# Setting up the folded weights of a tokenizer: query bias in two more columns, one semaphore for each bias, key projection ahead of the bias of V

## The chip, the cores and the metric

The kernel runs on one core of a Trainium2 chip. The metric is the device time of one launch in microseconds, the median of several executions. The kernel before takes 2070.14 us (median of 3 executions, 2069.56 to 2070.2).

## What is computed

The input is x, 2 batches of 4096 tokens of width 256, in float32. Three stages follow each other: a tokenizer with linear attention scores and a gate, an attention in which each token attends across the batch of 2, and a feed-forward part for the half of the tokens that a router picks. Only the first is touched by the change:

```
q = x @ Wq + bq
k = x @ Wk + bk
v = x @ Wv + bv
scores = jnp.einsum('btd,bsd->bts', q, k)
retained = jnp.einsum('bts,bsd->btd', d_gamma_batched * scores, v)
y = retained @ Wo + bo
out = jnp.where(y >= 0, y, prelu_a * y)
```

The kernel doesn't form q, k and v. It folds the weights once: A = Wk·Wqᵀ takes the place of the two projections in the score (x A xᵀ), Wv·Wo that of the value projection and the output projection, and the biases become a column added to the folded key (from Wq and bk), one extra column of the folded value (from Wk and bq, the term of the score that depends on the key token alone) and a row added to the value (from bv and Wo).

## The kernel before

It is written for one core with a program for each engine and semaphores between them: what stands in an engine's program is done in that order. The DMAs are issued by SP (SyncE), in its program's order too. Matrix products take float32 values in two halves: for each operand ScalarE (ACT) makes a rounded copy "hi" and VectorE (DVE) the rest "lo" = value minus hi, and TensorE (PE) does three products, hi·hi, hi·lo and lo·hi.

`setup_weights` (line 73) runs once, at the start of the launch. SP loads, in this order: the weights wqT, wkT, wvT and wo (256 KB each), the first chunk of x (512 KB, into x32), then two copies each of bq, bk and bv as columns (lines 98 to 101: four bytes per partition and half), the column of bo, and gamma, beta, attn_bo, prelu and wr, each a row that is copied to all 128 partitions. All of the biases and rows but wr count on one semaphore, `loaded`. PE forms the product pa = A (line 159, two banks) as soon as wqT and wkT are there, then pv = Wv·Wo (line 165). After that it waits for `rows`, with the bias products behind it: DVE makes bq_rows and bv_rows (a bias spread over 128 columns, lines 132 and 134), and waits ahead of them for all of `loaded`:

```
dve.wait_ge(loaded, 16 * n_loads)
...
pe.wait_ge(rows, 2 * KD)
```

Then PE does wkT·bq (line 171, into two more columns of pv), wqT·bk (line 174), bv_rows·wo (line 177) and bq_rows·bk (line 180), and only the last of these counts `prod` up, upon which DVE copies bk_col, vo_f and v_bias out of PSUM (lines 137 to 140), ACT makes vo_hi and DVE vo_lo. In between DVE has copied A out (a_f, line 122), ACT has split it (a_hi) and the first x (x_hi), and DVE made a_lo and x_lo. In float32 without halves, as in these set-up products, one matmul of the program stands in the trace as two records.

`tokenizer` (line 195) follows, for each of the two batches: `project` for 8 chunks of 512 tokens, then `attend` for 8 chunks. In `project`, PE does 12 matmuls of 512 columns with a_hi and a_lo (line 635: the folded key, two banks) and then 24 of 258 columns with vo_hi and vo_lo (line 648: the folded value, four banks); ACT and DVE copy the banks out with the bias and split them again. PE's first projection stands behind the bias products in its program. SP loads the x of a chunk two chunks ahead and, in chunk 0, the first four tiles of the gate. `attend` is the long part: per chunk 32 rounds of scores (line 678) and sums over values (line 663), with the gate streamed in. After the tokenizer come the attention weights, the mixing and the feed-forward part, which the change leaves alone.

Of the kernel before, what the change touches and what calls it, by code (L numbers as in the profile page):

```python
# [5 lines left out]
P = 128  # L6
# [9 lines left out]
F32 = mybir.dt.float32  # L16
# [56 lines left out]
def setup_weights(pr, W, ident, work):  # L73
# [3 lines left out]
    with ExitStack() as ctx:  # L77
        wqT, wkT, wvT, wo = (sb(nc, ctx, n, [P, KD, D]) for n in ("wqT", "wkT", "wvT", "wo"))
        bq2, bk2, bv2 = (sb(nc, ctx, n, [P, KD, 2]) for n in ("bq2", "bk2", "bv2"))
# [3 lines left out]
        pa, pv, (pb, pr_) = pr.banks[0:2], pr.banks[2:4], pr.banks[4:6]  # L83
        qk_loaded, vo_loaded, loaded, made, rows, prod, kept, hi_ok, lo_ok = (
            pr.sem("w_" + n) for n in ("qk_loaded", "vo_loaded", "loaded", "consts", "rows", "products", "kept",
                                       "hi", "lo"))
        n_loads = 3 * 2 + 1 + 4
# [4 lines left out]
        @block.sync  # L92
        def _(sp):
            for t, name, sem in ((wqT, "tok_WqT", qk_loaded), (wkT, "tok_WkT", qk_loaded),
                                 (wvT, "tok_WvT", vo_loaded), (wo, "tok_Wo", vo_loaded)):
                sp.dma_start(t[:, :, :], ins[name].rearrange("(k p) n -> p k n", p=P)).then_inc(sem, 16)
            sp.dma_start(x32, ins["xT"][0, 0]).then_inc(x_ld, 16)
            with nc.allow_non_contiguous_dma(reason="bias columns, once"):
                for t, name in ((bq2, "tok_bq"), (bk2, "tok_bk"), (bv2, "tok_bv")):
                    for j in range(2):  # L100
                        sp.dma_start(t[:, :, j], ins[name].rearrange("(k p) -> p k", p=P)).then_inc(loaded, 16)
                sp.dma_start(W["bo_col"][:, :], ins["tok_bo"].rearrange("(k p) -> p k", p=P)).then_inc(loaded, 16)
            sp.dma_start(W["gamma"][:, :], ins["attn_gamma"].partition_broadcast(P)).then_inc(loaded, 16)
            sp.dma_start(W["beta"][:, :], ins["attn_beta"].partition_broadcast(P)).then_inc(loaded, 16)
            sp.dma_start(W["attn_bo"][:, :], ins["attn_bo"].partition_broadcast(P)).then_inc(loaded, 16)
            sp.dma_start(W["prelu"][:, :], ins["tok_prelu_a"].partition_broadcast(P)).then_inc(loaded, 16)
            sp.dma_start(W["wr"][:, :], ins["ffn_wr"].partition_broadcast(P)).then_inc(pr.sem("wr_ld"), 16)

        @block.gpsimd
        def _(pool):  # L110
# [4 lines left out]
                                    base=0, pattern=[[-1, P]], channel_multiplier=1).then_inc(made, 1)  # L115

        @block.vector
        def _(dve):

            for j in range(KD):  # L120
                dve.wait_ge(prod, j + 1)
                nc.vector.tensor_copy(a_f[:, j, :], pa[j][:, 0:D]).then_inc(kept, 1)
            dve.wait_ge(hi_ok, 1)
            nc.vector.tensor_tensor(W["a_lo"][:, :, :], a_f[:, :, :], W["a_hi"][:, :, :].bitcast(F32),
                                    ALU.subtract).then_inc(lo_ok, 1)
            dve.wait_ge(x_hi_ok, 1)
            nc.vector.tensor_tensor(W["x_lo"][:, 0], x32, W["x_hi"][:, 0].bitcast(F32), ALU.subtract).then_inc(x_lo_ok, 1)
            dve.wait_ge(loaded, 16 * n_loads)
            dve.wait_ge(made, 3)

            for k in range(KD):
                nc.vector.tensor_scalar(bq_rows[:, k, :], ones[:, :], bq2[:, k, 0:1], None,
                                        ALU.mult).then_inc(rows, 1)
                nc.vector.tensor_scalar(bv_rows[:, k, :], ones[:, :], bv2[:, k, 0:1], None,
                                        ALU.mult).then_inc(rows, 1)
# [1580 lines left out]
```

## Time and profile before

| | |
|---|---|
| median of 3 executions | 2070.14 us |
| the profiled execution | 2072.95 us, of which its span is 2071.2 us |
| PE busy | 1988.7 us (96% of the span) |
| DVE, ACT, POOL busy | 1222.2, 675.0 and 451.0 us |
| bytes moved by DMA | 250.14 MB, mean 121 GB/s |
| chain that ended last, by engine | PE 90%, DVE 4%, issue 2%, ACT 2%, POOL 1% |
| costliest lines | L678 (scores) and L663 (values), 34% of the chain each |
| mean granted PE clock | 0.977 of full speed |

The page of the profile shows busy time for each engine and, in 40 slices, when. The chain of waits is followed back from the last instruction; it says which work the end hangs on. The timeline lists instructions in order of time, with the idle time of the engine before each in brackets and what ended it.
### The profile page before, as it was taken

What the parts mean: (1) busy time and instruction counts of PE and PEld (TensorE: products, weight loads), DVE (VectorE), ACT (ScalarE), POOL (GpSimd) and SP (SyncE); (2) the same over time, 40 slices, a digit from 0 to 9 for tenths busy, and PEclk for the clock granted to TensorE, in tenths of its full rate; (3) what the DMA queues carried; (4) which work ended last, traced back from release to release, by engine and by line L of the source; (5) the groups of instructions that cost most, each with busy time, mean ns of one, the idle gap of its engine ahead of it and who ended that gap; (6) DMA issues with size and microseconds to landing.
All of it is one profiled execution on the core that took longest, in us unless ns stands there. A gap on an engine that the chain in (4) does not pass through costs nothing.

```text
span 2071.2 us, 27479 instructions
## 1 busy us (share of the span) xinstructions
PE 1988.7 (96%) x9534; PEld 1646.7 (80%) x9534; DVE 1222.2 (59%) x2220; ACT 675.0 (33%) x1093; POOL 451.0 (22%) x578
## 2 busy tenths in 40 slices
PE   7999999999999999999999999999999989829998
PEld 6888888888888888888888888888887878718897
DVE  4656565665656556656565665656554358756553
ACT  4422222222222225422222222222222147524454
POOL 3302020202202023312020201202023057532342
PEclk9999999999999999999999999999999989959999
DMA  4232433334243333242433334243334469620110
GB/s 143 88 105 73 162 112 122 112 122 145 75 164 112 122 112 132 72 153 81 154 112 123 111 122 150 73 162 112 112 112 143 148 241 313 220 77 22 42 42 31
DMA packets 88114, 250.14 MB, mean 121 GB/s; under 512 B 11968, under 2 KB 32448, under 8 KB 88000
## 3 DMA queue, kind: packets, MB, share of 16 engines
q1 hardware_dynamic: 84928, 240.27, 34.5%
q0 software_dynamic: 3072, 8.44, 1.3%
q8 instruction: 61, 1.00, 0.2%
q14 instruction: 53, 0.43, 0.1%
HBM read 194.05 MB, written 54.62 MB: 120 GB/s over the span
## 4 chain that ended last, share of the span: by engine, by line
PE 90%; DVE 4%; issue 2%; ACT 2%; POOL 1%; DMA 0%; SPq 0%; DVEq 0%; ACTq 0%; POOLq 0%
PE bank L663 34%; PE bank L678 34%; PE bank L1568 4%; PE bank L810 4%; PE bank L1588 4%; PE bank L713 3%; PE bank L1169 2%; PE bank L635 1%; PE bank L609 1%; PE bank L619 1%; DVE kt L482 0%; DVE vf L493 0%; PE bank L648 0%; ACT work L380 0%; PE bank L836 0%
## 5 line engine op out<-in xcount | busy, mean ns | idle before, releaser
L678 PE MATMUL bank<-x_hi,kt 128*128 128x512 f32 x2048 | 724.0, 395 | 1.5 <-DVE work L519 1.4
L519 DVE SCALAR_TENSOR_TENSOR work<-bank,d_col,gate 128x512 f32<-128x512 f32 x512 | 383.8, 750 | 553.7 <-PE bank L678 544.7
L398 ACT ACTIVATE p_hi<-work 128x512 fp32r<-128x512 f32 x512 | 324.1, 633 | 1065.5 <-PE bank L663 1024.9
L678 PEld LDWEIGHTS bank<-x_hi,kt 128*128 128x128 f32 x2048 | 384.4, 188 | 90.4 <-DVE work L519 2.4
L663 PE MATMUL bank<-p_hi,v_hi 128*128 128x512 f32 x1024 | 407.0, 397 | 0.3 <-ACT yT L360 0.2
L663 PE MATMUL bank<-p_hi,v_lo 128*128 128x512 f32 x1024 | 404.2, 395 | 0.0
L663 PE MATMUL bank<-p_lo,v_hi 128*128 128x512 f32 x1024 | 403.4, 394 | 0.0
L678 PE MATMUL bank<-x_lo,kt 128*128 128x512 f32 x1024 | 401.0, 392 | 0.0
L507 DVE TENSOR_TENSOR p_lo<-work,p_hi 128x512 fp32r<-128x512 f32 x512 | 367.4, 718 | 29.3 <-ACT p_hi L398 29.2
L568 POOL TENSOR_SCALAR spread<-mv 128x4 f32<-128x4 f32 x16 | 4.9, 308 | 1125.4 <-DVE mv L451 1125.4
L663 PEld LDWEIGHTS bank<-p_hi,v_hi 128*128 128x128 f32 x1024 | 192.2, 188 | 50.6 <-DVE p_lo L507 5.3
L663 PEld LDWEIGHTS bank<-p_hi,v_lo 128*128 128x128 f32 x1024 | 192.3, 188 | 46.3
L663 PEld LDWEIGHTS bank<-p_lo,v_hi 128*128 128x128 f32 x1024 | 193.2, 189 | 44.7
L678 PEld LDWEIGHTS bank<-x_lo,kt 128*128 128x128 f32 x1024 | 192.3, 188 | 43.4
L1534 DVE TENSOR_TENSOR act_lo<-act,act_hi 128x512 fp32r<-128x512 f32 x64 | 59.2, 925 | 91.0 <-ACT act_hi L1472 90.8
L1568 PE MATMUL bank<-ffn,act_hi 128*128 128x256 f32 x512 | 97.4, 289 | 0.0
L1588 PE MATMUL bank<-fx_hi,ffn 128*128 128x512 f32 x256 | 92.5, 408 | 2.2 <-DVE fx_lo L1483 2.2
L1568 PEld LDWEIGHTS bank<-ffn,act_hi 128*128 128x128 f32 x512 | 84.2, 194 | 4.3 <-DVE act_lo L1534 0.2
L575 POOL TENSOR_TENSOR mn_sb<-mn_sb,gamma 128x256 f32<-128x256 f32 x64 | 55.2, 893 | 98.7 <-DVE mn_sb L456 98.7
L1568 PE MATMUL bank<-ffn,act_lo 128*128 128x256 f32 x256 | 73.6, 288 | 0.0
L713 PE MATMUL bank<-kt 128*128 128x256 f32 (+1 forms) x384 | 68.3, 339 | 2.2 <-DVE kt L544 2.2
L713 PEld LDWEIGHTS bank<-kt 128*128 128x128 f32 x384 | 59.2, 189 | 11.2 <-DVE kt L544 2.9
(226 smaller groups left out, 2271.7 us busy)
## 6 DMA issues: line engine op xcount, KB each, us to landing
gate<-in_gateT SPq DMA_DIRECT2D x256, 512.0 KB, 3.6
work<-in_xT SPq DMA_DIRECT2D x32, 512.0 KB, 4.7
scratch_rows<-rows SPq DMA_DIRECT2D x16, 518.0 KB, 4.0
scratch_h<-work SPq DMA_DIRECT2D x16, 512.0 KB, 3.0
scratch_mn<-mn_sb SPq DMA_DIRECT2D x16, 512.0 KB, 6.8
scratch_mT_hi<-mT_hi SPq DMA_DIRECT2D x16, 512.0 KB, 2.7
scratch_mT_lo<-mT_lo SPq DMA_DIRECT2D x16, 512.0 KB, 4.0
gate<-scratch_mn SPq DMA_DIRECT2D x16, 512.0 KB, 4.2
```

The costliest lines, as they stand in the source:

```text
L398: nc.scalar.activation(p_hi[:, i % 2, :], p32[:, i % RP, :], ACT.Copy).then_inc(hi_done, 1)
L507: nc.vector.tensor_tensor(p_lo[:, i % 2, :], p32[:, i % RP, :], p_hi[:, i % 2, :].bitcast(F32), ALU.subtract).then_inc(lo_done, 1)
L519: nc.vector.scalar_tensor_tensor(p32[:, i % RP, :], S[i % 2][:, :], d_col[:, i:i + 1], gate[:, g % RG, j, :], ALU.add, ALU.mult).then_inc( ...
L575: nc.gpsimd.tensor_tensor(mn_sb[:, j, :], mn_sb[:, j, :], W["gamma"][:, :], ALU.mult).then_inc(scaled, 1)
L663: mm = pe.matmul(Y[m][:, :], v, p, start=i == 0 and n == 0, stop=i == ST - 1 and n == 2)
L678: mm = pe.matmul(S[i % 2][:, :], w, x, start=n == 1, stop=n == 3 * KD)
L713: mm = pe.matmul(out, w, x, start=early(c, 1) and j == 0 and n == 0, stop=False, skip_group_check=True)
L810: mm = pe.matmul(bank[:, :], ww, x, start=i == 1, stop=i == 3 * pr.KD)
L1169: mm = pe.matmul(products[:, j, 0:D + 2], x, w, start=i == 0, stop=i == 3 * KD - 1)
L1534: nc.vector.tensor_tensor(a_lo[:, j % 2, :], act32[:, j % 2, :], a_hi[:, j % 2, :].bitcast(F32), ALU.subtract).then_inc(al_ok, 1)
L1568: mm = pe.matmul(YB[t // 2][:, (t % 2) * D:(t % 2 + 1) * D], a, w, start=j == 0 and t % 2 == 0 and n == 0, stop=j == FT - 1 and n == 2, sk ...
L1588: mm = pe.matmul(HB[j % 2][:, :], w, x, start=n == 1, stop=n == 3 * KD)
```

## The change

- The query bias gets two more columns behind the query weights: a tile wq_b of width D + 2 in place of wqT, with bq loaded into columns D and D + 1. The product of line 159 becomes 258 columns wide (line 157 of the changed kernel), and its last two columns are wkT·bq. The matmuls of line 171 are gone.
- Each set of bias columns has a semaphore (bq_ld, bk_ld, bv_ld) and is loaded by ACT's DMA queue at the start, five DMAs; bv once. x comes third on SP's queue, ahead of wvT and wo.
- The spread rows bq_rows and bv_rows are made by POOL, not by DVE.
- wqT·bk (line 163) stands before wvT·wo (line 169). The two products with the spread rows are a function `value_bias` that is called in PE's program behind the first key projection, ahead of the first value projection.
- bo's column, gamma, beta, attn_bo, prelu and wr are loaded in chunk 0 of `project`, behind the first four gate tiles, on a semaphore w_rows_ld that DVE waits for behind the last chunk of `project`.
- DVE makes x_lo before a_lo, and ACT x_hi before a_hi.

```diff
-        pa, pv, (pb, pr_) = pr.banks[0:2], pr.banks[2:4], pr.banks[4:6]
+        pa, pv, (pb, pr_) = pr.banks[0:2], pr.banks[2:4], pr.banks[6:8]
...
         @block.sync
-            for t, name, sem in ((wqT, "tok_WqT", qk_loaded), (wkT, "tok_WkT", qk_loaded),
-                                 (wvT, "tok_WvT", vo_loaded), (wo, "tok_Wo", vo_loaded)):
-                sp.dma_start(t[:, :, :], ins[name].rearrange("(k p) n -> p k n", p=P)).then_inc(sem, 16)
+            for t, name in ((wq_b[:, :, 0:D], "tok_WqT"), (wkT[:, :, :], "tok_WkT")):
+                sp.dma_start(t, ins[name].rearrange("(k p) n -> p k n", p=P)).then_inc(qk_loaded, 16)
             sp.dma_start(x32, ins["xT"][0, 0]).then_inc(x_ld, 16)
+            for t, name in ((wvT, "tok_WvT"), (wo, "tok_Wo")):
+                sp.dma_start(t[:, :, :], ins[name].rearrange("(k p) n -> p k n", p=P)).then_inc(vo_loaded, 16)
...
         @block.gpsimd
+            pool.wait_ge(bq_ld, 32)
+            pool.wait_ge(bv_ld, 16)
+            for k in range(KD):
+                nc.gpsimd.tensor_scalar(bq_rows[:, k, :], ones[:, :], wq_b[:, k, D:D + 1], None, ALU.mult).then_inc(rows, 1)
+                nc.gpsimd.tensor_scalar(bv_rows[:, k, :], ones[:, :], bv1[:, k, 0:1], None, ALU.mult).then_inc(rows, 1)
...
         @block.vector
             for j in range(KD):
                 dve.wait_ge(prod, j + 1)
+                nc.vector.tensor_copy(vo_f[:, j, D:D + 2], pa[j][:, D:D + 2])
                 nc.vector.tensor_copy(a_f[:, j, :], pa[j][:, 0:D]).then_inc(kept, 1)
+            dve.wait_ge(x_hi_ok, 1)
+            nc.vector.tensor_tensor(W["x_lo"][:, 0], x32, W["x_hi"][:, 0].bitcast(F32), ALU.subtract).then_inc(x_lo_ok, 1)
             dve.wait_ge(hi_ok, 1)
...
-            dve.wait_ge(loaded, 16 * n_loads)
...
+            dve.wait_ge(prod, KD + 3)
+            nc.vector.tensor_copy(W["v_bias"][:, :], pr_[:, 0:D + 2]).then_inc(kept, 1)
+            dve.wait_ge(kept, 2 * KD + 2)
...
         @block.scalar
+                for t, name, sem in ((wq_b[:, :, D], "tok_bq", bq_ld), (wq_b[:, :, D + 1], "tok_bq", bq_ld),
+                                     (bk2[:, :, 0], "tok_bk", bk_ld), (bk2[:, :, 1], "tok_bk", bk_ld),
+                                     (bv1[:, :, 0], "tok_bv", bv_ld)):
+                    act.dma_start(t, ins[name].rearrange("(k p) -> p k", p=P)).then_inc(sem, 16)
...
         @block.tensor
             pe.wait_ge(qk_loaded, 32)
+            pe.wait_ge(bq_ld, 32)
...
+                    mm = pe.matmul(pa[j][:, 0:D + 2], wkT[:, k, j * P:(j + 1) * P], wq_b[:, k, :], start=k == 0,
...
                     if early(c, 1):
+                        if b == 0:
+                            value_bias(pe)
                         pe.wait_ge(w_lo, 2)
```

PE's program from its first instruction to the first projection, before (a row is one or, with xN, N matmuls of the program; a_hi, a_lo are the halves of A, vo_hi, vo_lo those of Wv·Wo):

```order
L159 MATMUL bank<-wqT,wkT 128x256 x4
L165 MATMUL bank<-wo,wvT 128x256 x4
L171 MATMUL bank<-bq,wkT 128x2 x2
L174 MATMUL bank<-bk,wqT 128x2 x2
L171 MATMUL bank<-bq,wkT 128x2 x2
L174 MATMUL bank<-bk,wqT 128x2 x2
L177 MATMUL bank<-wo,bv_rows 128x256 x2
L180 MATMUL bank<-bk,bq_rows 128x2 x2
L602 UNCONDITIONAL_BRANCH
L635 MATMUL bank<-x_hi,a_hi 128x512
```

The same stretch of PE's program in the changed kernel, in two pieces, up to the first projection and from its last matmul on:

```order
L157 MATMUL bank<-wq_b,wkT 128x258 x4
L163 MATMUL bank<-bk,wq_b 128x2 x4
L169 MATMUL bank<-wo,wvT 128x256 x4
L609 UNCONDITIONAL_BRANCH
L642 MATMUL bank<-x_hi,a_hi 128x512
```

```order
L642 MATMUL bank<-x_hi,a_lo 128x512
L175 MATMUL bank<-wo,bv_rows 128x256 x2
L177 MATMUL bank<-bk,bq_rows 128x2 x2
L657 MATMUL bank<-vo_hi,x_hi 128x258
L657 MATMUL bank<-vo_lo,x_hi 128x258
```

Two products with the spread rows have moved from ahead of the 12 matmuls of the first key projection to behind them, wqT·bk from behind wvT·wo to ahead of it, and the two products with bq alone are gone.

DVE's program at the start, before:

```order
L122 COPY a_f<-bank 128x256 x2
L124 TENSOR_TENSOR a_lo<-a_f,a_hi 128x512
L127 TENSOR_TENSOR x_lo<-work,x_hi 128x1024
L132 TENSOR_SCALAR bq_rows<-ones_setup,bq 128x128
L134 TENSOR_SCALAR bv_rows<-ones_setup,bv 128x128
L132 TENSOR_SCALAR bq_rows<-ones_setup,bq 128x128
L134 TENSOR_SCALAR bv_rows<-ones_setup,bv 128x128
L137 COPY bk_col<-bank 128x2
L139 COPY vo_f<-bank 128x258 x2
L140 COPY v_bias<-bank 128x258
L142 TENSOR_TENSOR vo_lo<-vo_f,vo_hi 128x516
```

And DVE's program at the start in the changed kernel:

```order
L118 COPY vo_f<-bank 128x2
L119 COPY a_f<-bank 128x256
L118 COPY vo_f<-bank 128x2
L119 COPY a_f<-bank 128x256
L121 TENSOR_TENSOR x_lo<-work,x_hi 128x1024
L123 TENSOR_TENSOR a_lo<-a_f,a_hi 128x512
L126 COPY bk_col<-bank 128x2
L129 COPY vo_f<-bank 128x256 x2
L131 TENSOR_TENSOR vo_lo<-vo_f,vo_hi 128x516
L134 COPY v_bias<-bank 128x258
```

The four spread rows have left DVE, x_lo stands ahead of a_lo, two copies of two columns are new, and v_bias is copied last.

## Rows read from the trace of the kernel before

**Rows 1.** The page: busy us, share of the span and instructions of each engine.

```profile
PE 1988.7 (96%) x9534; PEld 1646.7 (80%) x9534; DVE 1222.2 (59%) x2220; ACT 675.0 (33%) x1093; POOL 451.0 (22%) x578
```

**Rows 2.** Chain of waits, first 110 us: start us, us, what.

```profile
8.83 6.65 DMA prelu<-in_tok_prelu_a
...
16.43 1.01 PE bank L171 x4
...
22.56 4.11 PE bank L635 x12
```

**Rows 3.** Timeline of PE: start us, us, instruction, records; brackets: idle before it.

```profile
4.49 3.69 PE L159 MATMUL bank<-wqT,wkT 128*128 128x256 f32 x8 [4.49 <-DMA wkT<-in_tok_WkT]
8.02 1.89 PE L165 MATMUL bank<-wo,wvT 128*128 128x256 f32 x8
16.43 1.01 PE L171 MATMUL bank<-bq,wkT 128*128 128x2 f32 x4 [6.52 <-DVE bv_rows L134]
17.30 0.99 PE L174 MATMUL bank<-bk,wqT 128*128 128x2 f32 x4
...
19.86 2.06 PE L177 MATMUL bank<-wo,bv_rows 128*128 128x256 f32 x4
...
22.42 0.77 PE L635 MATMUL bank<-x_hi,a_hi 128*128 128x512 f32 x1
...
25.09 0.40 PE L635 MATMUL bank<-x_hi,a_hi 128*128 128x512 f32 x1
...
26.50 0.28 PE L648 MATMUL bank<-vo_hi,x_hi 128*128 128x258 f32 x1
...
29.39 0.40 PE L635 MATMUL bank<-x_hi,a_hi 128*128 128x512 f32 x1
```

**Rows 4.** Windows: stretch, its length, each engine's busy us, then PEclk, DMA share, GB/s.

```profile
14.70:14.80 0.10, 0.00 (x0) 0.00 (x0) 0.00 (x0) 0.00 (x0) 0.00 (x0) 0.94 1.03 400
...
16.40:20.00 3.60, 3.57 (x17) 3.57 (x17) 0.00 (x0) 0.00 (x0) 0.00 (x0) 0.50 1.03 420
20.00:25.00 5.00, 5.00 (x15) 4.16 (x15) 1.86 (x5) 1.54 (x2) 0.00 (x0) 0.50 0.39 158
...
30.00:60.00 30.00, 30.00 (x189) 26.95 (x188) 22.07 (x36) 23.34 (x45) 20.29 (x41) 1.00 0.26 84
```

**Rows 5.** Timeline of DVE at the start.

```profile
8.22 0.42 DVE L122 COPY a_f<-bank 128x256 f32<-128x256 f32 x1 [1.19 <-PE bank L159]
9.34 0.69 DVE L124 TENSOR_TENSOR a_lo<-a_f,a_hi 128x512 fp32r<-128x512 f32 x1 [0.70 <-ACT a_hi L148]
10.29 1.22 DVE L127 TENSOR_TENSOR x_lo<-work,x_hi 128x1024 fp32r<-128x1024 f32 x1 [0.26 <-ACT x_hi L150]
...
22.68 0.75 DVE L139 COPY vo_f<-bank 128x258 f32<-128x258 f32 x2
```

**Rows 6.** Timeline of ACT at the start.

```profile
9.21 1.04 ACT L150 ACTIVATE x_hi<-work 128x1024 fp32r<-128x1024 f32 x1
23.46 0.64 ACT L152 ACTIVATE vo_hi<-vo_f 128x516 fp32r<-128x516 f32 x1 [13.21 <-DVE vo_f L139]
```

**Rows 7.** DMA issues in the first 60 us: count, KB each, us to landing.

```profile
bq<-in_tok_bq SPq DMA_DIRECT2D x2, 1.0 KB, 4.8
```

**Rows 8.** Line 97, load of the first x, issued at 2.82 us.

```profile
DMA to landing us min/median/max: 5.6/5.6/5.6
```

**Rows 9.** DMA from 7.5 to 8.0 us, the bias columns: packets, MB, share of 16 engines.

```profile
q1 hardware_dynamic: 774, 0.04, 105.3%
```

**Rows 10.** Groups of POOL instructions: count, busy us, mean ns, idle before.

```profile
L579 POOL TENSOR_TENSOR mn_sb<-mn_sb,beta 128x256 f32<-128x256 f32 x64 | 64.7, 1042 | 0.0
```

**Rows 11.** Timeline of all engines, first 60 us: SP's and POOL's start.

```profile
0.81 0.44 SPq L96 DMA_DIRECT2D wqT<-in_tok_WqT  x1
...
1.39 0.29 POOL L114 TENSOR_SCALAR_AFFINE_SELECT ident<-ident 128x128 f32<-128x128 f32 x1 [0.25 <-POOL ones_setup L112]
...
3.33 0.95 SPq L101 DMA_DIRECT2D bq<-in_tok_bq  x2
```

More of the change, by code:

```diff
@@ L82, in setup_weights @@
         a_f, vo_f = sb(nc, ctx, "a_f", [P, KD, D]), sb(nc, ctx, "vo_f", [P, KD, D + 2])
-        pa, pv, (pb, pr_) = pr.banks[0:2], pr.banks[2:4], pr.banks[4:6]
[L84 to L87, printed above, removed]
+        pa, pv, (pb, pr_) = pr.banks[0:2], pr.banks[2:4], pr.banks[6:8]
+        (qk_loaded, vo_loaded, bq_ld, bk_ld, bv_ld, made, rows, prod, kept, hi_ok, lo_ok) = (
+            pr.sem("w_" + n) for n in ("qk_loaded", "vo_loaded", "bq_ld", "bk_ld", "bv_ld", "consts", "rows", "products",
+                                       "kept", "hi", "lo"))
         x_ld, x_hi_ok, x_lo_ok = pr.sem("xp_ld0"), pr.sem("xp_hi"), pr.sem("xp_lo")
@@ L125, in _ @@
                                     ALU.subtract).then_inc(lo_ok, 1)
-            dve.wait_ge(x_hi_ok, 1)
-            nc.vector.tensor_tensor(W["x_lo"][:, 0], x32, W["x_hi"][:, 0].bitcast(F32), ALU.subtract).then_inc(x_lo_ok, 1)
-            dve.wait_ge(loaded, 16 * n_loads)
[L129 to L135, printed above, removed]
             dve.wait_ge(prod, KD + 1)
             nc.vector.tensor_copy(W["bk_col"][:, :], pb[:, 0:2 * KD:2]).then_inc(kept, 1)
+            dve.wait_ge(prod, KD + 2)
             for j in range(KD):
-                nc.vector.tensor_copy(vo_f[:, j, :], pv[j][:, 0:D + 2]).then_inc(kept, 1)
-            nc.vector.tensor_copy(W["v_bias"][:, :], pr_[:, 0:D + 2]).then_inc(kept, 1)
+                nc.vector.tensor_copy(vo_f[:, j, 0:D], pv[j][:, 0:D]).then_inc(kept, 1)
             dve.wait_ge(hi_ok, 2)
@@ L156, in _ @@
             pe.wait_ge(qk_loaded, 32)
+            pe.wait_ge(bq_ld, 32)
             for j in range(KD):
                 for k in range(KD):
-                    mm = pe.matmul(pa[j][:, 0:D], wkT[:, k, j * P:(j + 1) * P], wqT[:, k, :], start=k == 0,
+                    mm = pe.matmul(pa[j][:, 0:D + 2], wkT[:, k, j * P:(j + 1) * P], wq_b[:, k, :], start=k == 0,
                                    stop=k == KD - 1)
                 mm.then_inc(prod, 1)
+            pe.wait_ge(bk_ld, 32)
+            for j in range(KD):
+                for k in range(KD):
+                    mm = pe.matmul(pb[:, 2 * j:2 * j + 2], wq_b[:, k, j * P:(j + 1) * P], bk2[:, k, :],
+                                   start=j == 0 and k == 0, stop=k == KD - 1, skip_group_check=True)
+            mm.then_inc(prod, 1)
             pe.wait_ge(vo_loaded, 32)
@@ L182, in _ @@
             last.then_inc(prod, 1)
+        return value_bias
 def gram_view(work, D):
@@ L310, in project @@
                             load_gate(0, b * NC, g)
+                    if early(c, 1) and b == 0:
+                        for n, name in (("gamma", "attn_gamma"), ("beta", "attn_beta"), ("attn_bo", "attn_bo"),
+                                        ("prelu", "tok_prelu_a")):
+                            sp.dma_start(W[n][:, :], ins[name].partition_broadcast(P)).then_inc(pr.sem("w_rows_ld"), 16)
+                        with nc.allow_non_contiguous_dma(reason="a bias column, once"):
+                            sp.dma_start(W["bo_col"][:, :], ins["tok_bo"].rearrange("(k p) -> p k", p=P)).then_inc(
+                                pr.sem("w_rows_ld"), 16)
+                        sp.dma_start(W["wr"][:, :], ins["ffn_wr"].partition_broadcast(P)).then_inc(pr.sem("wr_ld"), 16)
                 chunks(sp, b, project)
```

43 lines of the change are left out of this document (14 added, 29 removed).

## Prediction

> **What bounds the kernel now.** I read the busy times of the page first: PE works in 96% of the span and no other engine in more than 59% [rows 1]. So the launch is PE's work one after the other, and a change gains only what PE waits for or does slowly. The change lies in the set-up. The chain of waits says what holds the start: a DMA, the load of prelu, which lands at 15.5 us, then the bias products from 16.43 us, then the first projection, line 635 [rows 2]. None of the products behind the wait needs prelu, or the three broadcast rows ahead of it; they hang on it because all count on one semaphore. In PE's timeline the reader sees the hole: work from 4.49 us, idle for 6.52 us before line 171, the first projection at 22.42, the first value product (line 648) at 26.50 [rows 3]. From there the projections run without a gap, PE 30.00 of 30 us busy [rows 4]. That start, 26.50, is the number to follow: what comes behind it is the same work in the same order, and I let it shift as a whole.
>
> The same rows show two speeds. Line 159 has 8 records from 4.49 until line 165 starts at 8.02, a pitch of 0.44 us for 256 columns; line 165 has the same shape and goes through 8 in 1.89, 0.236 each [rows 3]. So the clock rose from 1.2 to 2.4 GHz close to 8.0. It fell within 14.7 to 14.8, with PE idle since 9.91, and stood at 0.50 until about 25 [rows 4]: six of the twelve first projections went at 0.445 (22.42 to 25.09), six at 0.235 (25.09 to 26.50) [rows 3].
>
> **The change, part by part.**
>
> *Start of PE.* Before, PE starts when wkT has landed, 4.49 [rows 3]. Now it waits for both columns of bq too. They are the first two issues of ACT's queue. No row shows a DMA issued by ACT; SP issues such a column in 0.48 (0.95 for two) and its queue begins at 0.81 [rows 11], so I let the second go out at 1.29. A bq column took 4.8 us to land, behind five large loads on one queue [rows 7]; that gives an upper end of 1.29 + 4.8 = 6.1. The lower end is 4.49, if the columns are there before wkT. A column is 256 packets of four bytes, and 774 small packets took all 16 engines 0.5 us [rows 9], so a column takes 0.17. If bq and bk pass between the packets of wqT and wkT, wkT is late by up to 4 · 0.17 = 0.7; with the two of bq, by 0.35. I take 4.9, near the lower end, since the columns have a queue without a backlog; the range keeps 4.49 to 6.1. The Trainium skill (DMA: Bandwidth & Descriptors, Rules for kernel authors) says that spreading DMAs over the issuing engines saves only issue time, since all run on the same 16 engines and interleave. By that rule the columns do delay wkT and 4.9 is right; if the queues did not share, it would be 4.49 and the whole sum 0.4 better.
>
> *PE's own products.* Line 157: 8 records, 258 instead of 256 columns, 3.53 · 258/256 = 3.56 at the low clock, until 8.46. The two more columns cost 0.03 us and do away with 8 records of line 171, at a pitch of 0.22 (16.43 to 17.30 for four [rows 3]) 1.7 us. Line 163: 8 two-column records, 0.22 each at 1.2 GHz; at 2.4 GHz nothing shows them, between 0.11 (half) and 0.22; I take 0.11, since nothing but the clock would hold them: 0.9, until 9.4. Line 169: 8 · 0.236 = 1.9 at 2.4 GHz, until 11.3. Its operand wo is now the last of the five large loads, the place that x had, which landed at 2.82 + 5.6 = 8.4 [rows 8]; with five columns in between (5 · 0.17) 9.3, just under 9.4. That cover is thin: each us beyond costs one.
>
> *A and x in halves.* The second a_f copy started 0.2 us after line 159's last record, at 8.22 [rows 5]; now 8.7. Two two-column copies are added, one in the wait for the second product, one at under 0.42 ahead of a_f; say 9.1 for a_f's end. Then x_lo, 1.22, and a_lo, 0.69 [rows 5]: 11.0. x_hi (1.04 [rows 6]) must be ready by 9.1: x is third on the queue instead of fifth, so not later than 8.4, and x_hi ends by 9.5 at the latest, x_lo by 10.7, a_lo by 11.4. So DVE and PE end together, DVE 0.3 ahead. Before, a_lo and x_lo ended at 11.5 [rows 5], to no use.
>
> *First projection.* It starts at 11.3 instead of 22.42. If the clock rose at the end of line 157 and stays, 12 · 0.235 = 2.8, until 14.1; before, 4.08.
>
> *Bias of V.* Behind it value_bias: 4 records of 256 columns and 4 of two, 4 · 0.236 + 4 · 0.11 = 1.4, until 15.5. It waits for the spread rows, from POOL. No POOL row has this shape; between a 128x128 select at 0.29 [rows 11] and a tensor-tensor of 128x256 at 1.04 [rows 10], four take 1.2 to 4.2. The third bias, fifth on ACT's queue, goes out by 0.81 + 5 · 0.48 = 3.2 and at 4.8 lands by 8.0, so the rows stand by 12.2, under 14.1. POOL has nothing else to do there.
>
> *Value halves.* vo_f follows line 169: 11.3 + 0.75 for two copies [rows 5], vo_hi 0.64 [rows 6], vo_lo 0.7: 13.5, under 15.5. The copy of v_bias waits for value_bias, and queued behind it on DVE is x_lo of chunk 1: 15.6 + 0.4 + 1.2 = 17.2. PE wants that after 24 value products, (29.39 − 26.50) = 2.9 [rows 3], at 18.4. The first vf copies stand behind x_lo too, some 0.8 later against line 648 than before; four banks take that up, and DVE is busy for 22 of 30 us there [rows 4], so it catches up.
>
> *Rows loaded late.* Six issues, 0.48 each, 2.9 on SP's queue behind the gate tiles and ahead of the load of chunk 3's x. PE needs that chunk three chunks of 36 · 30.00/189 = 5.7 us after chunk 0 [rows 4]; cost nothing, with some 8 us of cover. They are first read in `attend`.
>
> *Sum.* With 0.1 for the edge between engines the first value product moves from 26.50 to 15.6, 10.9 us: the idle time 6.5, line 171 1.7, line 174 0.8 (1.7 to 0.9), lines 177 and 180 1.2 (2.6 to 1.4), the first projection 1.3 (4.1 to 2.8), less 0.4 for the later start, 0.1 for the edge and 0.03 for the wider product. Against the profiled execution (span 2071.2, 2072.95 in all) that is 2062.1; its surplus of 2.8 over the median of 2070.14 I leave out on both sides: 2070.14 − 10.9 = **2059.2 us**.
>
> **The rivals.** *The clock rises late (chance 0.22).* The first rise came after 3.5 us of 256-column products. The second came only 8.6 us after line 171 began, behind 3.6 us of two-column and 1.9 us of 256-column products and some 2.6 of 512 [rows 3, 4]. What made the second so late the rows don't tell, but two-column products stood in front of it, and line 163 now puts some right where the rise may fall. If it is missed, line 163 costs 1.7 and line 169 8 · 0.44 = 3.5: the first projection starts at 8.46 + 1.7 + 3.5 = 13.7, and with the clock up about there V starts at 18.0: gain 8.5, 2061.6. If PE starts at 6.1 and the first projection goes low too (12 · 0.445 = 5.3), V starts at 6.1 + 3.56 + 1.7 + 3.5 + 5.3 + 1.4 = 21.6: gain 4.9, 2065.2. The Trainium skill (TensorE: Matmul & The Clock Gate, What's actually happening) says that the gate's watch runs free and isn't reset by a kernel's start; by that the rise moves from one execution to the next and both cases would appear. This trace is one execution and can't show it.
>
> *The columns come late (0.11).* ACT's issue is slower than SP's, or small packets hold up wkT for longer: PE starts at 6.1. All behind moves by 1.2: gain 9.7 at the high clock, or wo is late by as much; 2060.4 to 2062.
>
> *The gain is given back (0.05).* The change moves the first projection, but the next waits take its place: chunk 1 stalls on x_lo, or the late rows crowd x out. For a result within 0.2% (4.1 us) 6.8 of 10.9 must go; the covers above are 1.2 and some 8 us, so two of them must fail.
>
> *Slower (0.01).* PE stays at 1.2 GHz through the projections because the set-up breaks its work into pieces. A chunk takes 5.7 at the high clock and, at 0.445 against 0.235 for the 512-column products and twice for the others, about 11.1 at the low: 5.4 lost each. With the third chunk the 10.9 are gone; three make 2070.14 − 10.9 + 16.2 = 2075.4. The longest low stretch in these rows is some 10 us, and it held the idle hole that the change removes, so this is a remote end.
>
> **How the numbers follow.** The forecast with its own spread (PE starting at 4.49 to 5.2, two-column records at 0.11 to 0.22, DVE or PE last) has 0.61 and lies at 2058.8 to 2061; the others as given. The likeliest gives 2059.2. The range must leave out 2 in 10 at most: from 2058.2 (0.4 from an early wkT, 0.6 for the spread of the median) to 2064.5 it holds the forecast, nearly all of the late clock and of the late columns. About 0.2% is what a measurement of this kernel tells from no change; faster by more has 0.94, within 0.05, slower 0.01.
>
> **What would show it.** In the changed profile: line 157 starts at 4.5 to 5.2 on wkT or bq; line 163 ends by 9.5 and line 169 by 11.4, at a pitch of 0.236; no wait of PE on DVE longer than 0.4 before line 642; line 642's twelve records at 0.235; value_bias with no wait on POOL; the first record of line 657 at 15.6. Pitches of 0.44 in line 169 mean the late clock. A start of line 157 past 5.5 means the columns. A wait of PE between 15.6 and 30 means that a cover failed. The prediction is wrong if line 657 starts at 15.6 and the whole is still not some 11 us shorter: then work behind it isn't merely shifted.

## The result, and the profile after

The changed kernel takes 2063.75 us (median of 7, 2062.0 to 2064.71) against 2070.2 for the kernel before, a ratio of 0.9964 with a 95% interval of 0.9953 to 0.9974: it is faster by 5.4 to 9.7 us. Two repeats in later measurements gave 0.996 (0.9947 to 0.9974 and 0.9946 to 0.9974), medians 2061.7 and 2061.85. The forecast was 2059.2 us with a range of 2058.2 to 2064.5: direction and range held, and the size, 10.9 us, was too large: by the ratios the gain is 7.5 us in the first measurement and 8.3 in the repeats.

PE's timeline of the changed kernel answers to [rows 3] (start us, us, instruction, records; in brackets the idle time before and what ended it):

```profile
6.41 3.78 PE L157 MATMUL bank<-wq_b,wkT 128*128 128x258 f32 x8 [6.41 <-DMA wq_b<-in_tok_bq]
9.98 1.71 PE L163 MATMUL bank<-bk,wq_b 128*128 128x2 f32 x8
11.54 3.76 PE L169 MATMUL bank<-wo,wvT 128*128 128x256 f32 x8
14.74 0.99 PE L642 MATMUL bank<-x_hi,a_hi 128*128 128x512 f32 x1
15.53 0.47 PE L642 MATMUL bank<-x_lo,a_hi 128*128 128x512 f32 x1
15.84 0.39 PE L642 MATMUL bank<-x_hi,a_lo 128*128 128x512 f32 x1
...
18.16 1.02 PE L175 MATMUL bank<-wo,bv_rows 128*128 128x256 f32 x4
19.02 0.50 PE L177 MATMUL bank<-bk,bq_rows 128*128 128x2 f32 x4
19.39 0.36 PE L657 MATMUL bank<-vo_hi,x_hi 128*128 128x258 f32 x1
```

The hole of 6.52 us is gone, and PE starts later: at 6.41 on the bq columns, where 4.9 was expected. Line 169 still goes at the low clock (3.76 us against the 1.9 expected), and the clock rises only inside the first projection: the starts from 15.84 on are 0.23 apart. The first value product (line 657) comes at 19.39, not at 15.6.

From there on I had shifted everything as a whole. The stretch of the projections did not stay the same, though. The first score product, with which `attend` begins, stood 43.2 us behind the first value product before:

```profile
69.73 0.47 PE L678 MATMUL bank<-x_hi,kt 128*128 128x512 f32 x1
```

In the changed kernel, with the starts of three chunks of the projections ahead of it:

```profile
39.45 0.47 PE L642 MATMUL bank<-x_hi,a_hi 128*128 128x512 f32 x1
...
45.57 0.50 PE L642 MATMUL bank<-x_hi,a_hi 128*128 128x512 f32 x1 [0.19 <-DVE x_lo L432]
...
51.77 0.50 PE L642 MATMUL bank<-x_hi,a_hi 128*128 128x512 f32 x1 [0.24 <-DVE x_lo L432]
...
63.80 0.47 PE L687 MATMUL bank<-x_hi,kt 128*128 128x512 f32 x1
```

That is 44.4 us behind 19.39, and PE waits for DVE's x_lo on the way. From the second chunk on, PE's chunks start 5.69 us apart up to 39.45, and 6.12, 6.20 and 6.10 behind that. In the kernel before these steps are 5.69 or 5.70, but for the last, 5.97. ACT's x_hi, from which x_lo is made, shows the pace (timeline of ACT, one row a chunk):

```profile
36.81 1.04 ACT L382 ACTIVATE x_hi<-work 128x1024 fp32r<-128x1024 f32 x1
43.07 1.06 ACT L382 ACTIVATE x_hi<-work 128x1024 fp32r<-128x1024 f32 x1
49.21 1.04 ACT L382 ACTIVATE x_hi<-work 128x1024 fp32r<-128x1024 f32 x1
```

A chunk takes ACT and DVE together 6.1 to 6.3 us here, 5.9 in two more of its steps, and PE 5.7 where it doesn't wait. Neither is busy all the time; they wait for each other: between 19 and 64 us DVE waits 9.1 us for x_hi, and ACT 11.9 us for vf. So PE runs ahead of a chain that is slower than it, until the lead is used up; how long that lasts depends on when DVE begins with chunk 0. Its first step there is vf, the copy of the folded value out of PSUM with the bias added, and that begins late (timeline of DVE, the changed kernel and then the kernel before):

```profile
19.57 0.43 DVE L134 COPY v_bias<-bank 128x258 f32<-128x258 f32 x1 [2.07 <-PE bank L177]
20.24 1.23 DVE L432 TENSOR_TENSOR x_lo<-work,x_hi 128x1024 fp32r<-128x1024 f32 x1 [0.25 <-DVE v_bias L134]
21.38 0.42 DVE L499 TENSOR_TENSOR vf<-bank,v_bias 128x258 f32<-128x258 f32 x1
```

```profile
27.41 0.43 DVE L493 TENSOR_TENSOR vf<-bank,v_bias 128x258 f32<-128x258 f32 x1 [1.11 <-PE bank L648]
```

vf starts 2.0 us behind the first value product; before, 0.9.

There is a second difference. DVE's kt is the lo half of the folded key, two for each chunk; POOL's v_lo is the lo half of the folded value. DVE's second kt of the fourth chunk, in the changed kernel and then in the kernel before:

```profile
40.65 1.18 DVE L488 TENSOR_TENSOR kt<-work,kt 128x512 f32 x1
```

```profile
47.06 0.68 DVE L482 TENSOR_TENSOR kt<-work,kt 128x512 f32 x1
```

POOL's v_lo began at 40.53, ahead of this kt, in the changed kernel, and at 47.07, with it, in the kernel before. In all fourteen profiles of this document, over the eight chunks of the first batch, a kt takes 0.68 to 0.70 us when no v_lo of POOL began before it, and 1.05 to 1.22 when one did and is still running. ACT's step over this chunk is 6.26 us (36.81 to 43.07); in both profiles of the kernel before it is 5.77. So POOL has a part in the pace of ACT and DVE.

Three marks serve for all that follows: the start of PE on the weights, the first value product V, and the first score product S. The rest is the span from S to its end.

| kernel | PE start | V | S | S minus V | rest |
|---|---|---|---|---|---|
| before | 4.49 | 26.50 | 69.73 | 43.2 | 2001.5 |
| before, again (c3_before) | 4.30 | 28.13 | 71.40 | 43.3 | 1997.7 |
| changed | 6.41 | 19.39 | 63.80 | 44.4 | 1998.3 |
| changed, again (c1_after) | 6.01 | 16.47 | 60.89 | 44.4 | 1998.9 |
| changed, again (c2_after) | 6.31 | 16.78 | 61.18 | 44.4 | 1998.8 |

### The profile page after: what moved, and what is told of

Read it like the earlier page. It is cut to its first block, busy times and chain, and to the rows that moved or that the text cites. A ratio compares the mean times of both kernels' runs of the same rounds, so it can differ in the third digit from the quotient of the medians.

```text
span 2062.1 us, 27464 instructions
## 1 busy us (share of the span) xinstructions
PE 1983.2 (96%) x9526; PEld 1641.2 (80%) x9526; DVE 1223.3 (59%) x2218; ACT 675.1 (33%) x1093; POOL 457.0 (22%) x582
## 4 chain that ended last, share of the span: by engine, by line
PE 91%; DVE 4%; issue 2%; ACT 1%; POOL 1%; DMA 0%; DVEq 0%; ACTq 0%; POOLq 0%
PE bank L672 35%; PE bank L687 34%; PE bank L1577 4%; PE bank L819 4%; PE bank L1597 4%; PE bank L722 3%; PE bank L1178 2%; PE bank L642 1%; PE bank L616 1%; PE bank L626 1%; PE bank L657 1%; DVE kt L488 1%; DVE vf L499 0%; ACT work L386 0%; PE bank L845 0%
## 5 line engine op out<-in xcount | busy, mean ns | idle before, releaser
L687 PEld LDWEIGHTS bank<-x_lo,kt 128*128 128x128 f32 x1024 | 192.3, 188 | 43.3
```

The costliest lines, as they stand in the source:

```text
L687: mm = pe.matmul(S[i % 2][:, :], w, x, start=n == 1, stop=n == 3 * KD)
```

## The experiments

Theory: three things took the missing microseconds. Small packets on ACT's queue hold the weights up; the clock rises late; and DVE's order behind the value bias costs, since ACT and DVE and not PE pace the projections. Rivals: the load order holds the weights, the clock is harmless since DVE's chain ends last anyway, and PE paces the projections.

**The changed kernel again** (no edit).

> The changed kernel again, as the measure for the runs beside it. Expected as in its first profile: line 157 starts at 6.4 us on the bq columns, line 169 at a pitch near 0.44 us or 0.236 us as the clock rises late or early, the first value product (line 657) at 19.4 us (16 to 20), the first score product (line 687) at 63.8 us, and 6 to 9 us less than the kernel before.

Median 2061.7, ratio 0.996 (0.9947 to 0.9974). Its PE timeline differs from the first one in the clock:

```profile
6.01 3.78 PE L157 MATMUL bank<-wq_b,wkT 128*128 128x258 f32 x8 [6.01 <-DMA wq_b<-in_tok_bq]
9.58 1.20 PE L163 MATMUL bank<-bk,wq_b 128*128 128x2 f32 x8
10.64 1.97 PE L169 MATMUL bank<-wo,wvT 128*128 128x256 f32 x8
```

The same program, the start 0.4 earlier, and line 169 takes 1.97 instead of 3.76, the rise having come in line 163; V is 2.9 earlier. So a late rise costs 2.5 us (2.9 less the 0.4 of the start), and both occur.

**No bias columns at all** (POOL sets the biases to zero, so the run leaves the tokenizer's biases out):

```diff
+            nc.gpsimd.memset(wq_b[:, :, D:D + 2], 0.0).then_inc(bq_ld, 1)
+            nc.gpsimd.memset(bk2[:, :, :], 0.0).then_inc(bk_ld, 1)
+            nc.gpsimd.memset(bv1[:, :, :], 0.0).then_inc(bv_ld, 1)
...
-                    act.dma_start(t, ins[name].rearrange("(k p) -> p k", p=P)).then_inc(sem, 16)
...
```

> The changed kernel without the five loads of bias columns: the three biases are set to zero on POOL, so this run leaves the biases of the tokenizer out. Theory: small packets on ACT's queue hold up the weights on SP's queue, and that is what makes PE start at 6.4 us. Then line 157 starts at 4.4 to 4.7 us, everything behind it up to the first value product is some 1.7 to 1.9 us earlier (more if the clock also rises earlier), and the time is 1.5 to 2 us below the changed kernel. Rival: wkT is late because x is now third on SP's queue and the engines share among the large loads; then line 157 still starts near 6 us and the time stays within 0.5 us of the changed kernel.

```profile
4.71 3.62 PE L155 MATMUL bank<-wq_b,wkT 128*128 128x258 f32 x8 [4.71 <-DMA wkT<-in_tok_WkT]
```

PE starts at 4.71; V 15.09, S 59.03, median 2059.99 against 2061.7 beside it. The rival falls: with x third on the queue too, wkT comes in time. S minus V is 43.9, not 44.4: the kt of the fourth chunk takes 0.68 here, and ACT's step over it 5.76. It takes 0.68 in the kernel before too, and in the run with the semaphore alone, further down; in the ten profiles with bias columns on ACT's queue it takes 1.17 to 1.21. How the columns bring this about is not shown.

How the queues share is seen in the DMA rows of 3 to 4.5 us, first of the changed kernel, then of this one (packets, MB, share of 16 engines; q1 is SP's queue, q10 ACT's):

```profile
q1 hardware_dynamic: 230, 0.22, 45.2%
q10 hardware_dynamic: 236, 0.00, 8.4%
```

```profile
q1 hardware_dynamic: 362, 0.51, 102.4%
```

With both queues in use the engines are busy for 54% together (62% in the first repeat of the changed kernel), and the weights move at less than half the rate. It isn't the time of the small packets (8.4%) that is missing but what lies between the packets.

**A warm clock**: five matmuls of 512 columns at PE's start.

```diff
+            nc.vector.memset(a_f[:, :, :], 1.0).then_inc(pr.sem("w_warm"), 1)
...
+            for i in range(5):
+                pe.matmul(pr.banks[4][:, :], a_f[:, 0, 0:P], a_f[:, :, :].rearrange("p k n -> p (k n)"), start=True, stop=True)
             pe.wait_ge(qk_loaded, 32)
```

> The changed kernel with five matmuls of 512 columns on a tile set to one, at the start of PE's program while it waits for the weights, into a bank that nothing reads. Theory: the low clock through lines 157, 163 and 169 and the start of the first projection costs 1.6 + 0.7 + 1.4 + 0.6 us. With the clock up at 6.4 us, line 157 takes 1.9 us instead of 3.6, line 169 goes at 0.236, and the first value product comes at 15 to 16 us instead of 19.4; the time is 3 to 4 us below the changed kernel. Rival: DVE's and ACT's chain, not PE, sets the start of the projections; then PE waits for x_lo or a_lo ahead of line 642, the first value product comes at 17.5 us or later, and less than 2 us is gained.

```profile
1.52 6.06 PE L156 MATMUL bank<-a_f 128*128 128x512 f32 x10 [1.52 <-DVE a_f L115]
7.41 1.91 PE L161 MATMUL bank<-wq_b,wkT 128*128 128x258 f32 x8
```

The weights' product takes 1.91 instead of 3.78, as expected, but the ten records last until 7.4 and hold it up by a microsecond. V came at 15.82: 3.6 before the profile with the late rise, 0.65 before the one with the early rise. The median of 2061.41 is no different from the repeat's 2061.7 within their spread. So the theory holds for V, and the 3 to 4 us of time did not appear. The run beside it had an early rise in its profile, against which only 0.65 at V was left to gain. How often the rise is early is not shown: of the six profiles here with five columns on ACT's queue and no matmuls of ones, three have it early (the two repeats and the next run) and three late (the first profile, and two runs further down).

**x_lo of chunk 1 ahead of v_bias** on DVE:

```diff
+            dve.wait_ge(x_hi_ok, 2)
+            nc.vector.tensor_tensor(W["x_lo"][:, 1], query_tiles(work, KD)[1], W["x_hi"][:, 1].bitcast(F32),
+                                    ALU.subtract).then_inc(x_lo_ok, 1)
             dve.wait_ge(prod, KD + 3)
...
```

> The changed kernel with DVE's x_lo of chunk 1 moved ahead of the copy of v_bias. Theory: the projections are paced by ACT and DVE (6.1 us for a chunk) and not by PE (5.7), so that what counts is when DVE starts on vf of chunk 0; behind v_bias and x_lo that is 21.38 us, 2.0 us after the first value product. With x_lo made before, vf starts at 20.2 to 20.5 us, the first score product comes 0.8 to 1.1 us earlier than in the changed kernel at the same start of the value products, and the time falls by about 1 us. Rival: PE sets the pace and DVE catches up; then the first score product stands as far behind the first value product as in the changed kernel (44.4 us) and the time does not move.

```profile
14.97 1.23 DVE L134 TENSOR_TENSOR x_lo<-work,x_hi 128x1024 fp32r<-128x1024 f32 x1 [0.26 <-ACT x_hi L385]
16.56 0.43 DVE L137 COPY v_bias<-bank 128x258 f32<-128x258 f32 x1 [0.36 <-PE bank L180]
17.41 0.43 DVE L502 TENSOR_TENSOR vf<-bank,v_bias 128x258 f32<-128x258 f32 x1 [0.42 <-PE bank L660]
```

V 16.38, vf 1.0 behind it, S 59.94: S minus V is 43.6 instead of 44.4, with V where the changed kernel has it at an early rise. PE's chunks stay 5.69 to 5.76 apart for two steps more than in the changed kernel. The theory holds: ACT and DVE pace this stretch. In the median (2061.18) the gain of 0.8 us is lost in the spread.

**The semaphore alone**, in the kernel before:

```diff
-                        sp.dma_start(t[:, :, j], ins[name].rearrange("(k p) -> p k", p=P)).then_inc(loaded, 16)
+                        sp.dma_start(t[:, :, j], ins[name].rearrange("(k p) -> p k", p=P)).then_inc(pr.sem("w_cols_ld"), 16)
...
-            dve.wait_ge(loaded, 16 * n_loads)
+            dve.wait_ge(pr.sem("w_cols_ld"), 16 * 6)
...
```

For the other five loads DVE waits behind the last chunk of `project`.

> The kernel before with one thing changed: the six loads of bias columns count on a semaphore of their own, and DVE waits for that ahead of the spread rows; for bo's column, gamma, beta, attn_bo and prelu it waits behind the last chunk of project. All loads stay on SP's queue in the same order. Theory: the wait for prelu is 4.0 us of the hole; the columns have landed by 9.7 us, DVE comes from x_lo at 11.5, so line 171's products start at 12.4 instead of 16.4 us, the first value product at 22 to 22.5 instead of 26.5, and the time falls by 3.5 to 4.5 us. Rival: the semaphore is nearly all of it, since an earlier start also keeps the clock up; then the first value product comes at 20.5 us or before and 6 us or more are gained.

```profile
12.48 0.61 PE L171 MATMUL bank<-bq,wkT 128*128 128x2 f32 x4 [2.44 <-DVE bv_rows L134]
12.95 0.59 PE L174 MATMUL bank<-bk,wqT 128*128 128x2 f32 x4
...
16.17 0.77 PE L636 MATMUL bank<-x_hi,a_hi 128*128 128x512 f32 x1
...
18.44 0.40 PE L636 MATMUL bank<-x_hi,a_lo 128*128 128x512 f32 x1
...
20.07 0.29 PE L649 MATMUL bank<-vo_hi,x_hi 128*128 128x258 f32 x1
```

The rival was right: ratio 0.9965 (0.9953 to 0.9978), median 2063.24. The products start at 12.48 as reckoned, 4 us earlier, while the clock is still up; two-column records go at 0.115 where they took 0.22. The clock does fall, at 15.0 (granted 1.00 before, 0.50 behind), and rises again about 18.4, so that five of the twelve first projections go low against six before. V comes at 20.07 and S at 63.32, sooner than in the profile of the changed kernel with the late rise (63.80). One semaphore brings about the whole gain that the change had there; the profiles with the early rise are 2.1 to 2.4 us ahead of it at S.

**The value bias ahead of the first projection again**:

```diff
+            pe.wait_ge(rows, 2 * KD)
+            for k in range(KD):
+                pe.matmul(pr_[:, 0:D], bv_rows[:, k, :], wo[:, k, :], start=k == 0, stop=k == KD - 1, skip_group_check=True)
...
-                            value_bias(pe)
...
```

> The changed kernel with its third part undone: the two products with the spread rows stand ahead of the first key projection again. Theory: POOL's spread rows are ready at 14.6 us only, since bv lands at 10.9 us, and the first key projection is what hides them; PE now waits for POOL behind wvT times wo (from 12.3 us if the clock rose early, hardly at all if late) and the first value product comes at 18.5 to 19.5 us whatever the clock does, up to 2.5 us later than in the repeat of the changed kernel. Rival: the order is neutral; no wait of PE on POOL, the first value product within 0.3 us of where the same clock puts it in the changed kernel, and DVE, which has v_bias earlier, starts on vf 1 us sooner.

Median 2062.92, ratio 0.9964 (0.995 to 0.9978). The profile had a late rise (14.5 us), wvT·wo ended at 14.8 and POOL's rows were there by 14.6, so PE did not wait: V 18.90, and S minus V 43.7, so S 62.60. That is 1.2 us before the changed kernel at its late rise. Of it 0.5 lies in V, where the clock, up by 14.8, had risen about 1 us sooner than there (inside the first projection, 15.6). The other 0.7 lies behind V and belongs to the order: v_bias and x_lo are done by 19.0, and vf starts 0.9 behind V, as in the kernel before. The run can't tell the order apart at an early rise; the next does, with three of the matmuls of ones:

> The products with the spread rows ahead of the first key projection, as two runs above, and three matmuls of 512 columns on a tile of ones at PE's start, so that the clock is up early. Theory: only at the high clock does the third part of the change matter; the spread rows come at 14.6 us (bv landing at 10.9, then 3.5 us of POOL), wvT times wo ends near 11.6, so PE waits some 3 us on POOL, and the first value product comes at 18.5 to 19 us, against 15.8 with the first key projection in front; 2 to 3 us lost. Rival: the order is worth nothing at either clock; PE waits less than 0.5 us on POOL and the first value product stands at 15.5 to 16.2 us.

```profile
9.72 1.97 PE L173 MATMUL bank<-wo,wvT 128*128 128x256 f32 x8
13.45 1.13 PE L177 MATMUL bank<-wo,bv_rows 128*128 128x256 f32 x4 [1.75 <-POOL bv_rows L111]
```

PE waits 1.75 us for POOL's rows, V 17.65 against 15.82 in the warm kernel with the projection in front (five matmuls of ones there, but its line 169 starts within 0.3 of this one's), S 61.35 against 60.22. So the third part of the change gains about 1.1 us at S when the clock is up early. That is less than the 2 to 3 expected, since POOL's rows were there at 13.4 and not at 14.6, and v_bias is out of DVE's way (S minus V 43.7). It loses about 0.7 when the clock is late.

**The two more columns undone**:

```diff
-                    mm = pe.matmul(pa[j][:, 0:D + 2], wkT[:, k, j * P:(j + 1) * P], wq_b[:, k, :], start=k == 0,
+                    mm = pe.matmul(pa[j][:, 0:D], wkT[:, k, j * P:(j + 1) * P], wq_b[:, k, 0:D], start=k == 0,
...
+                    mm = pe.matmul(pv[j][:, D:D + 2], wkT[:, k, j * P:(j + 1) * P], wq_b[:, k, D:D + 2], start=False,
+                                   stop=k == KD - 1, skip_group_check=True)
...
```

The wait on bq's columns moves along, to in front of the second of these products.

> The changed kernel with its first part undone: the product of the weights has 256 columns again and doesn't wait for bq, and wkT times bq is made by eight two-column records behind wvT times wo, as before. Theory: wkT itself lands at 6.0 us, as late as bq, so line 155 or so starts 0.1 to 0.4 us earlier only, and the eight records (0.115 each at the high clock, 0.2 at the low one) put the first projection 0.5 to 1.5 us later at the same clock; the two more columns are worth about 1 us. Rival: the wait on bq is what holds the start; then PE starts at 4.5 to 5 us and the first value product comes at least 0.5 us earlier than in the changed kernel.

```profile
6.08 3.78 PE L155 MATMUL bank<-wq_b,wkT 128*128 128x256 f32 x8 [6.08 <-DMA wkT<-in_tok_WkT]
...
14.71 0.95 PE L172 MATMUL bank<-wq_b,wkT 128*128 128x2 f32 x8
```

wkT itself lands at 6.08, while the changed kernel starts on bq at 6.41, 6.01 and 6.31 in its three profiles: the wait on bq costs 0.3 at most. The eight records take 0.81 at the high clock. V 19.62, S 64.04, 0.24 behind the changed kernel, both at a late rise. Median 2063.31 (0.9966, 0.9954 to 0.9977) against 2061.85 of the repeat beside it. The first projection starts 0.8 later (15.52 against 14.74), inside the expected 0.5 to 1.5, but then runs wholly at the high clock: the clock rose about 1 us sooner than in the changed kernel's profile, which is worth some 0.4 (an estimate: where the value bias stood in front, the same lead of the clock put V 0.5 earlier at the same start). So the two columns are worth between 0.2 and 0.7 at S, under the 1 us expected; the run doesn't say it more closely.

> The changed kernel once more, beside the two runs above: 7 to 10 us less than the kernel before; line 157 from 6.0 to 6.4 us; the first value product at 16.5 us if line 169 runs at a pitch of 0.236, and at 19.4 us if it runs at 0.44; the first score product 44.4 us behind it in both cases.

Median 2061.85; an early rise again, with the marks in the table.

**Together.** Three matmuls of ones and x_lo first, both as above:

> The changed kernel with x_lo of chunk 1 ahead of v_bias on DVE and with three matmuls of 512 columns on a tile of ones at PE's start (five lasted until 7.4 us and held line 157 up by 1 us). Theory: the gains add: line 157 starts at 6.0 to 6.6 us at a pitch of 0.22, the first value product comes at 14.7 to 15.5 us and the first score product 43.5 us behind it, at 58.2 to 59; against the repeat of the changed kernel 1.5 to 2.5 us less, and it no longer depends on when the clock rises. Rival: DVE's x_lo and a_lo or the load of wo take over; then PE waits ahead of line 642 and the first value product stays at 15.8 us or later.

```profile
9.04 1.05 PE L170 MATMUL bank<-bk,wq_b 128*128 128x2 f32 x8 [0.58 <-DMA bk<-in_tok_bk]
```

V 15.79, S 59.34, median 2059.63, ratio 0.9949 (0.9935 to 0.9963). V was expected at 15.5 at the latest: a further wait appeared, on bk's columns, which land at 9.0. Last, the same with three columns instead of five and two matmuls of ones; POOL sets the second column of bq and of bk to zero and makes the rows of bq before it waits for bv:

```diff
...
-                for t, name, sem in ((wq_b[:, :, D], "tok_bq", bq_ld), (wq_b[:, :, D + 1], "tok_bq", bq_ld),
-                                     (bk2[:, :, 0], "tok_bk", bk_ld), (bk2[:, :, 1], "tok_bk", bk_ld),
-                                     (bv1[:, :, 0], "tok_bv", bv_ld)):
+                for t, name, sem in ((wq_b[:, :, D], "tok_bq", bq_ld), (bk2[:, :, 0], "tok_bk", bk_ld),
+                                     (bv1[:, :, 0], "tok_bv", bv_ld)):
...
```

> As the run before (with two such matmuls at the start), and with three loads of bias columns instead of five: the second column of bq and of bk, which nothing reads in the end, is set to zero on POOL; POOL makes the rows of bq before it waits for bv. Theory: packets on ACT's queue slow the weights on SP's in proportion, so with 3 of 5 columns and one of bq ahead instead of two, line 157 starts at 5.0 to 5.6 us, and the first value product comes at 14 to 14.8 us. Rival: it is not the number of packets but that two queues are active at all; then line 157 starts at 6 us as before and nothing is gained over the run before.

```profile
5.48 2.01 PE L167 MATMUL bank<-wq_b,wkT 128*128 128x258 f32 x8 [0.53 <-DMA wkT<-in_tok_WkT]
7.33 0.95 PE L173 MATMUL bank<-bk,wq_b 128*128 128x2 f32 x8
8.63 1.99 PE L179 MATMUL bank<-wo,wvT 128*128 128x256 f32 x8 [0.35 <-DMA wo<-in_tok_Wo]
```

PE starts at 5.48, V 14.47, S 58.02; median 2058.24, ratio 0.9941 (0.9927 to 0.9955). It is the fastest of all, 12 us under the kernel before, and in its median 3.5 us under the repeats of the changed kernel, though the intervals of the ratios overlap. The start follows the number of columns: none 4.71, three 5.48, five 6.0 to 6.4. With PE this early, wo is the next load that it waits for (0.35).

**The kernel before again** (no edit).

> The kernel before, profiled a second time. In its first profile 2001.5 us lie between the first score product (69.73) and the end of the span (2071.2); in the profiles of the changed kernel and its variants, where that work is the same, 1996.9 to 2000.8. Theory: this rest moves from one execution to the next by a few us, since the clock falls and rises in the stages behind the tokenizer; so the first score product is at 68 to 70 us again and the rest comes out somewhere in 1997 to 2001. Rival: the late loads or the order of the change do something for the work behind too; then the rest stays at 2001 to 2002.

S 71.40 (later than the 68 to 70 expected), rest 1997.7. So the rest isn't tied to the change: it ran from 1996.9 (x_lo first and warm) to 2001.5 us (the first profile of before) over all profiles. What moves it is not shown. A gain of S shows in a single time only within some 4.6 us.

## Why the prediction was right in direction and too large

By its own steps:

- *The hole goes and the path shortens*: right. Over the profiles, S falls from 69.7 and 71.4 to 60.9, 61.2 and 63.8, a mean of 70.6 to 62.0: 8.6 us, in line with the 5.4 to 9.7 measured. The semaphore alone (S 63.32) accounts for 7.2 of it.
- *Start of PE*: the term was mis-sized. I took 4.9 by counting the time of the small packets (0.17 us a column, from [rows 9]) and kept 6.1 as the upper end. Measured 6.0 to 6.4, past that end in two of three profiles: the columns cost 1.3 to 1.7 us (4.71 without them). The step that failed is the conversion of packets into delay: [rows 9] shows packets that had long been queued on one queue, and on two queues the engines stood idle for nearly half the time. The rule of the Trainium skill that I set beside it (DMA: Bandwidth & Descriptors, Rules for kernel authors), that the issuing engines' DMAs interleave on the same engines, points the right way; that it costs more than the packets' own time is what the runs add.
- *The clock*: the late rise was a rival at 0.22. It stood in the first profile (2.5 us by the repeat), not in the other two. The sentence of the Trainium skill that the gate's watch runs free of the kernel's start (TensorE: Matmul & The Clock Gate, What's actually happening) fits in kind, since the rise isn't tied to the start. It doesn't fit in size: the half microsecond of play that the section names is far less than the some 5 us between the two rises here, in the same program with starts 0.4 us apart. What held it back in the first profile stays open. That the two-column records keep it down, as I half suggested, isn't shown: in both repeats it rose in the middle of line 163. The price of such a record at the high clock, 0.11, was right (0.115).
- *Value halves*: this step was wrong. I wrote that vf would be late by 0.8 and that DVE, busy for 22 of 30 us, catches up. vf was late by 1.1 and DVE never caught up: S minus V rose by 1.2 in every profile of the changed kernel. Of this 0.7 is vf: it goes when vf starts 0.9 behind V again (43.7, the value bias in front), and with x_lo moved S minus V falls by 0.8. The other 0.5 is the slower kt of the fourth chunk, which I had no term for: without it S minus V is 43.9, with vf as late as ever. The misreading was in [rows 4]: PE "30.00 of 30 us busy" with DVE and ACT at three quarters looks like a PE-bound stretch. But ACT and DVE wait for each other (x_hi, x_lo, vf, v_hi in turn), and the chain of them takes 5.8 to 6.3 us a chunk; PE only had a lead, which in the kernel before lasted to the last chunk. The chain of waits of the kernel before said so: between the first and the last of the rows below stands no step of PE. I read it up to the first projection only.

```profile
26.69 0.69 ACT work L380
27.38 0.53 ACT kt L384
...
73.49 1.66 PE bank L678 x6
```

- *Rows for value_bias, rows loaded late, wo*: the covers held. POOL's rows came at 14.6 (12.2 expected; the first took 1.8 us and three more 0.6 each, and bv landed at 10.9 where I had 8.0) under a projection that ended later too. At the early rise the cover was 1.0 us (14.2 and 14.5 in the repeats, against 15.24 and 15.56).

From the forecast S of 58.8 (69.73 − 10.9) to 63.80 in the first profile: 1.5 for the start, 2.3 for the clock and the edges up to V (19.39 against 15.6 in all), 1.2 behind V; 5.0 in sum. In the first repeat, with the early rise, it is 0.9 up to V and 1.2 behind it.

The range held, but not by the forecast's own path: none of the three medians lies in the 2058.8 to 2061 that had 0.61. The first profile shows the late clock, the late columns and the loss behind V together, though the prediction priced the first two as rivals and the third at nothing; that the time still came out 0.8 under the upper end is in part luck.

## What to carry to other kernels

Give every group of loads that is waited for by itself a semaphore of its own before moving anything: here that alone was most of the gain. A busy engine of 100% is no proof that it sets the pace; look for two other engines that hand work to each other, and compare the step of their chain with its pitch. Column loads of four-byte elements on a second DMA queue are not free beside weights that PE waits for: load fewer of them (loading them later was not tried).

## What the runs showed of the hardware

- Two DMA queues in use, one of them with four-byte packets: 54% and 62% of the 16 engines' time used from 3 to 4.5 us in two profiles with five columns, 85% with three, against 102% with one queue. What fills the gaps (making the packets, or switching) stays open.
- The clock's rise moved by some 5 us between executions of the same program, and a set-up of short products is worth 2.5 us more or less by it. Matmuls on a constant tile during the wait for the weights made line 157's product take 1.91 instead of 3.78 us. With the semaphore alone the clock fell at 15.0, behind an idle time of 2.44 us that ended at 12.48, two-column products from there to 14.29 and 256-column products since.
- The five float32 matmuls of 512 columns at the start of the warm kernel are ten records and took 6.06 us, partly at either clock level; a record of 512 columns on the rounded halves takes 0.235 at the high one.
- DVE's kt (128x512) took 0.68 to 0.70 us, and 1.05 to 1.22 where a v_lo of POOL had begun before it and was still running; where the two began together, kt took 0.68 and POOL's v_lo 1.25 to 1.27 instead of 0.64 to 0.75. What they share, the traces don't say.
- The first POOL tensor-scalar of the launch took 1.80 us in the first profile and the next three 0.6 each. Over the profiles the first took between 0.6 and 2.2, by no order that the runs show.
